# A vision transformer block on one core: for the first four images the unturned scores ahead of the turned ones, and the last q and k pair ahead of their denominators

## The chip, the cores and the metric

The kernel runs on one core of one Trainium2 chip. The metric is the device time of one execution in microseconds (us). Engines are named as in the profile: PE is TensorE (PEld its weight loads), DVE is VectorE, ACT is ScalarE, POOL is GpSimd, SP is SyncE, which only issues transfers here. Each engine runs its own instruction stream in order, and streams meet in semaphores.

## What is computed

A patch embedding with quantised weights gives 16 images of 37 tokens of width 256. On them stand an attention block and a mixture-of-experts attention block. The change lies in the first attention block. There, numerator and denominator come from two different sets of scores: the numerator from queries and keys turned by position (rotary), the denominator from the same queries and keys unturned. The causal mask is put on afterwards, on the numerator alone.

```python
qkv = x @ Wqkv                       # 16 heads of width 16
q_rot, k_rot = _rotate(q, cos, sin), _rotate(k, cos, sin)
num = jnp.exp(jnp.einsum('bhqd,bhkd->bhqk', q_rot, k_rot) * scale)
den = jnp.sum(jnp.exp(jnp.einsum('bhqd,bhkd->bhqk', q, k) * scale), axis=-1, keepdims=True)
attn = jnp.where(causal, num / den, 0.0)
y = jnp.einsum('bhqk,bhkd->bhqd', attn, v)
out = y @ Wout + bout
```

After it come residual, layer norm, the second block's q, k and gates, eight value experts, a second attention, and a sum over 32 pairs of head pair and expert (the long tail of the kernel, which the change does not touch).

## The kernel before

**Stages.** 0 to about 37 us: embedding, layer norm, turning of x. 34 to about 54 us: projections q, k, v of the first block. 48 to about 77 us: its attention, in four blocks `b` of four images. From there on: the second block, with PE nearly full to the end.

**Projections.** `PJ` lists twelve jobs in order, `NPJ` = 12: q and k of half 0 (images 0 to 7), 128 columns of the width at a time (jobs 0 to 3), v (4, 5), q and k of half 1, first 128 columns (6, 7), v (8, 9), q and k of half 1, second 128 columns (10, 11, "the last q and k pair"). They go to PSUM banks `PJB` = 0 to 7 and then 4 to 7 again. `proj_job(n)` is the PE part, `proj_read(n)` the ACT part (L575): for q and k two copies into `qun` or `kun` (L587), for v four into `vblk` (L596). Each adds one to `act_read`.

**Rotation.** `rope(r)` (L882) runs on DVE, once for each half and 128 columns: a shuffle, two products, a sum, and two writes each to `qrot` and `krot` (L899 to L906). It waits for ACT's read of its k job. `rope(0)` and `rope(1)` give what turned scores of blocks 0 and 1 need, `rope(2)` and `rope(3)` serve blocks 2 and 3.

**Attention of a block.** On PE: `scores(b, 0)` (turned) and `scores(b, 1)` (unturned), 32 matmuls each, both into banks 0 to 3, two banks for each half `t`; `attend(b)`, 64 small matmuls with v; `denominators(b)`, 8 records of matmuls with a matrix of ones. On ACT: `exps(b, 0)` into `en` (two buffers), `exps(b, 1)` into `ed` (one buffer), two instructions each (L648). On DVE: `causal(b)` masks `en` (L913, two instructions), `denominators(b)` takes the reciprocal (L930), `normalise(b)` writes `yT` (L935).

**Order on PE** (L1291 on): scores(0,0), job 10, job 11, scores(0,1), attend(0); scores(1,0), denominators(0), scores(1,1), attend(1); scores(2,0), denominators(1), scores(2,1), attend(2); scores(3,0), denominators(2), scores(3,1), output projection of the first groups (`out_proj`, L1274), denominators(3), more output projection, attend(3).

**Order on ACT** (L650 on): reads 0 to 9, exps(0,0), reads 10 and 11, exps(0,1), `ve_hi(0)` (an expert's weights rounded, L657), exps(1,0), exps(1,1), `ve_hi(1)`, exps of blocks 2 and 3.

**Order on DVE** (L918 on): rope(0), rope(1), rope(2), causal(0), rope(3); causal(1), denominators(0), normalise(0), causal(2), denominators(1), normalise(1), denominators(2), normalise(2), causal(3).

The order is written out by hand. `exp_ready` counts ACT's exponentials in the order in which they are issued, `s_ps` PE's halves of scores.

Of the kernel before, what the change touches and what calls it, by code (L numbers as in the profile page):

```python
# [23 lines left out]
KC = D // P  # L24
# [89 lines left out]
def vit_block(nc, x, tokw, vecs, consts, wqkv, wout, w2, ve, oe, mask_rows, out):  # L114
    with ExitStack() as ctx:
        def sem(name):
            return ctx.enter_context(nc.semaphore(name))
# [15 lines left out]
        NVR = 2  # L133
# [80 lines left out]
        qk = ExitStack()  # L214
# [8 lines left out]
        late = range(NOE, NOR)  # L223
# [30 lines left out]
        sm = {n: sem(n) for n in names}  # L254

        def cols(name, rows=P):
            a, b = _C[name]
            return cst[0:rows, a:b]
# [15 lines left out]
        def qk_set(hf, c):  # L274
            return [("qk", hf, c, kind) for kind in range(2)]

        PJ = qk_set(0, 0) + qk_set(0, 1) + [("v", m, 0, 0) for m in range(NV // 2)] + qk_set(1, 0)
        PJ += [("v", m, 0, 0) for m in range(NV // 2, NV)] + qk_set(1, 1)
        NPJ, NEARLY = len(PJ), KC * 2
        PJB = [0, 1] + [2, 3] + [4, 5] + [6, 7] + [4, 5] + [6, 7]  # L280
        PJPREV = [max([m for m in range(n) if PJB[m] == PJB[n]], default=-1) for n in range(NPJ)]
        RSTEPS = 8

        def act_reads(n):

            return n + 1

        def rope_reads(n):

            return RSTEPS * (len([j for j in PJ[:n] if j[0] == "qk"]) // 2) + 2  # L290

# [244 lines left out]
        def _(act):  # L536
# [38 lines left out]
            def proj_read(n):  # L575

                what, a, c, kind = PJ[n]
                act.wait_ge(sm["proj1_ps"], n + 1)
                if what == "qk":
                    if n == 0:  # L580

                        act.wait_ge(sm["qb_ready"], G)
                    im = slice(a * B // 2, (a + 1) * B // 2)
                    src = ps[:, PJB[n], 0:QH].rearrange("p (i s) -> p i s", s=SE)[:, :, 0:S]
                    for j in range(2):
                        dst = kun[:, c, im, DH2 * j:DH2 * j + S] if kind else qun[:, c, im, j]
                        ins = act.activation(dst, src, ACT.Copy, scale=cols("par")[:, (0 if kind else 4) + j:][:, 0:1])  # L587
                else:
                    if a == 0:

                        act.wait_ge(sm["vblk_zero"], 1)
                    for ii in range(2):
                        src = ps[DH2 * ii:DH2 * ii + S, PJB[n], :].rearrange("p (i a x) -> p i a x", a=2, x=P)
                        for p_ in range(2):
                            dst = vblk[DH2 * p_:DH2 * p_ + S, NVI * a + ii:NVI * (a + 1):2, :, p_]
                            ins = act.activation(dst, src[:, :, p_].rearrange("p i (h d) -> p i h d", d=DH1), ACT.Copy)  # L596
                ins.then_inc(sm["act_read"], 1)
# [36 lines left out]
            def exps(b, kind):  # L634

                if kind == 0 and b >= 2:
                    act.wait_ge(sm["pv_ps"], b - 1)
                if kind == 1 and b >= 1:
                    act.wait_ge(sm["den_ps"], b)
                for t in range(2):  # L640
                    act.wait_ge(sm["s_ps"], 4 * b + 2 * kind + t + 1)
                    src = ps[0:QR, 2 * t:2 * t + 2, 0:KC * 2 * JS * S]
                    if kind == 0:
                        dst = en[:, b % 2, t].rearrange("p r c i j s -> p r (c i j s)")
                    else:
                        src = src.rearrange("p r (c x) -> p r c x", c=KC)
                        dst = ed[:, :, :, 2 * t:2 * t + 2].rearrange("p r c i j s -> p r c (i j s)")
                    act.activation(dst, src, ACT.Exp, scale=DH1 ** -0.5).then_inc(sm["exp_ready"], 1)  # L648

            for n in range(NPJ - 2):  # L650
                proj_read(n)

            def ve_hi(e):
                act.wait_ge(ve_in[e % NVR], 16 * (e // NVR + 1))
                if e >= NVR:
                    act.wait_ge(sm["ve_ps"], NT * (e - NVR + 1))
                act.activation(vehi[:, e % NVR], veraw[:, e % NVR], ACT.Copy).then_inc(sm["vehi_ready"], 1)  # L657

            for b in range(NB):
                exps(b, 0)  # L660
                if b == 0:
                    proj_read(NPJ - 2)
                    proj_read(NPJ - 1)
                exps(b, 1)
                if b < NVR:
                    ve_hi(b)
            def x2_hi(g):

                act.wait_ge(sm["x2T_ps"], g + 1)
# [93 lines left out]
        def _(dve):  # L763
# [144 lines left out]

            def causal(b):
                for t in range(2):  # L910
                    dve.wait_ge(sm["exp_ready"], 4 * b + t + 1)
                    v = en[:, b % 2, t].rearrange("p r c i j s -> p (r c i j) s")
                    dve.tensor_tensor(v, v, bcast(cols("keep", QR), 1, 2 * KC * JP),  # L913
                                      ALU.mult).then_inc(sm["en_ready"], 1)
# [3 lines left out]
            rope(1)  # L918
            rope(2)
            causal(0)  # L920
            rope(3)

# [189 lines left out]
        def _(pe):  # L1112
# [101 lines left out]
            def scores(b, kind):  # L1214

                late = b * BI * 2 // B + 1
                pe.wait_ge(sm["keys_zero"], 2)
                pe.wait_ge(sm["rope_t"], RSTEPS * KC * late)
                pe.wait_ge(sm["act_read"], act_reads(PJ.index(("qk", late - 1, KC - 1, 1))))
                if b == kind == 0:  # L1220
                    bank_free(NEARLY - 1)
                for t in range(2):
                    if b + kind:
                        pe.wait_ge(sm["exp_ready"], 4 * b + 2 * kind + t - 1)
                    for ii in range(2):
                        i = b * BI + 2 * t + ii
                        for c in range(KC):
                            o = (c * 2 + ii) * JS * S
                            for r in range(RT):
                                rows = slice(r * P // RT, (r + 1) * P // RT)  # L1230
                                key = (kun if kind else krot)[rows, c, i]
                                qry = (qun if kind else qrot)[rows, c, i].rearrange("p a b -> p (a b)")
                                ins = pe.matmul(ps[0:QR, 2 * t + r, o:o + JS * S], key, qry, start=True, stop=True)  # L1233
                    ins.then_inc(sm["s_ps"], 1)

            def attend(b):
                if b < 2:
                    bank_free(NPJ - 3 if b == 0 else NPJ - 1)
                if b >= 2:
                    pe.wait_ge(sm["yT_ready"], b - 1)  # L1240
                for ii in range(BI):
                    if ii % 2 == 0:
                        pe.wait_ge(sm["en_ready"], 2 * b + ii // 2 + 1)
                    if b == NB - 1 and ii == 2:
                        turn_x2(0)
                    for c in range(KC):
                        u = c * BI + ii
                        for j in range(JP):
                            vv = vblk[:, b * BI + ii, c * JP + j].rearrange("p a b -> p (a b)")
                            ins = pe.matmul(ps[32 * j:32 * j + 32, 4 + 2 * (b % 2), u * S:(u + 1) * S], vv,  # L1250
                                            en[:, b % 2, ii // 2, j // JS, c, ii % 2, j % JS], start=True, stop=True)
                ins.then_inc(sm["pv_ps"], 1)

            def denominators(b):
                pe.wait_ge(sm["exp_ready"], 4 * b + 4)
                if b < 2:
                    bank_free(NPJ - 3 if b == 0 else NPJ - 1)
                if b >= 2:
                    pe.wait_ge(sm["yT_ready"], b - 1)
                for j in range(JP):  # L1260
                    ins = pe.matmul(ps[32 * j:32 * j + 32, 5 + 2 * (b % 2), 0:UN * S], cols("blk2", QR),
                                    ed[:, j // JS, :, :, j % JS], start=True, stop=True)
                ins.then_inc(sm["den_ps"], 1)
# [25 lines left out]
                ins.then_inc(sm["x2T_ps"], 1)  # L1289

            for b in range(NB):  # L1291
                scores(b, 0)
                if b == 0:
                    proj_job(NPJ - 2)
                    proj_job(NPJ - 1)
                else:
                    denominators(b - 1)
                scores(b, 1)
                if b == NB - 1:
                    out_proj(0)  # L1300
                    out_proj(1)
                    denominators(b)
                    for g in range(2, NOP):
                        out_proj(g)
                attend(b)
# [253 lines left out]
```

## Time and profile before

| what | value |
|---|---|
| runs | 240.1, 241.33, 242.55 us; median 241.33 |
| the profiled execution | 240.91 us, its span 238.4 us |
| mean granted clock of PE | 0.979 |
| PE busy | 207.9 us of the span (87%) |
| DVE busy | 178.7 us (75%) |
| ACT busy | 93.7 us (39%) |
| POOL busy | 79.5 us (33%) |

The span is the stretch in which the profile has instructions; 2.51 us of the profiled execution's time lie around it. The page divides the span into 40 slices and gives the busy share of each engine and the clock that was granted to PE. The chain that ended last is followed back from the last instruction: what stands in it sets the time, and what does not has slack. Idle time before an instruction comes with the instruction that ended it.

### The profile page before, as it was taken

To read this page: it belongs to the slowest core of one execution; us is meant where nothing else is said; L and a number is where in the kernel's file an instruction comes from. 1 tells how busy PE (TensorE), PEld (TensorE's weight loads), DVE (VectorE), ACT (ScalarE), POOL (GpSimd) and SP (SyncE) were. 2 spreads that over 40 slices of the span, in tenths; PEclk is the share of its full clock that TensorE was granted. 3 is DMA by queue.
4 is the path that set the end of the run, shared out by engine and by line. 5 is a ranking of instruction groups with operands and counts; after the bars stand their busy time and mean duration, and the time that the engine had idled before them with its cause. 6 is when DMAs were issued, how large, how long until landed. Compare 5 with 4: busy or idle time off the path is not lost.

```text
span 238.4 us, 5151 instructions
## 1 busy us (share of the span) xinstructions
PE 207.9 (87%) x2079; PEld 179.6 (75%) x2079; DVE 178.7 (75%) x324; ACT 93.7 (39%) x184; POOL 79.5 (33%) x82
## 2 busy tenths in 40 slices
PE   0153969689979799999999999999999999999994
PEld 0033849688865689987677777778989999999993
DVE  1679895998977767933558666775799979979972
ACT  3578739958741335445332155156202022110000
POOL 8562677000443424002253564955661000000000
PEclk9999999979999679999999999999999999999999
DMA  6998000000000010001602006067005435532102
GB/s 177 265 302 322 2 0 4 0 3 3 3 3 3 18 71 3 0 0 29 252 3 88 3 12 254 0 181 201 3 7 185 120 123 172 165 95 61 44 0 103
DMA packets 7181, 19.56 MB, mean 82 GB/s; under 512 B 1043, under 2 KB 1878, under 8 KB 7030
## 3 DMA queue, kind: packets, MB, share of 16 engines
q1 hardware_dynamic: 7158, 19.24, 26.3%
q8 instruction: 16, 0.26, 0.5%
q14 instruction: 7, 0.06, 0.1%
HBM read 18.55 MB, written 0.68 MB: 81 GB/s over the span
## 4 chain that ended last, share of the span: by engine, by line
PE 49%; DVE 28%; issue 9%; ACT 4%; POOL 4%; DMA 4%; SPq 1%; DVEq 0%; ACTq 0%; POOLq 0%
PE ps L265 13%; PE ps L266 11%; PE ps L267 11%; DVE gx L1101 7%; DMA tw<-tok_weight 4%; PE ps L1233 3%; PE ps L1274 2%; PE ps L1434 2%; DVE oelo L1075 2%; DVE rden L930 2%; DVE amax L774 1%; PE ps L1404 1%; ACT ptb L720 1%; DVE stat L803 1%; POOL velo L485 1%
## 5 line engine op out<-in xcount | busy, mean ns | idle before, releaser
L1101 DVE TENSOR_TENSOR gx<-maskb,oT 128x1184 fp32r<-128x1184 bf16 x31 | 42.3, 1414 | 0.6 <-PE ps L267 0.6
L1038 DVE COPY_PREDICATED v<-onehot,ps 128x512 f32<-128x512 uint8 (+3 forms) x40 | 25.7, 661 | 17.6 <-PE ps L267 17.3
L265 PE MATMUL ps<-gx,oelo 128*128 128x296 f32 x124 | 37.8, 305 | 0.6 <-DVE gx L1101 0.6
L267 PE MATMUL ps<-gx,oehi 128*128 128x296 f32 x124 | 37.2, 300 | 0.0
L266 PE MATMUL ps<-gx,oehi 128*128 128x296 f32 x124 | 37.0, 298 | 0.0
L265 PE MATMUL ps<-vehi,x2lo 128*128 128x512 f32 (+3 forms) x90 | 35.2, 392 | 0.0
L266 PE MATMUL ps<-velo,x2hi 128*128 128x512 f32 (+3 forms) x90 | 33.3, 370 | 0.0
L267 PE MATMUL ps<-vehi,x2hi 128*128 128x512 f32 (+3 forms) x90 | 33.2, 369 | 0.0
L485 POOL TENSOR_TENSOR velo<-veraw,vehi 128x1024 fp32r<-128x1024 f32 x8 | 19.1, 2390 | 23.8 <-ACT vehi L657 17.3
L265 PEld LDWEIGHTS ps<-gx,oelo 128*128 128x128 f32 x124 | 23.3, 188 | 1.8 <-issue 1.3
L266 PEld LDWEIGHTS ps<-gx,oehi 128*128 128x128 f32 x124 | 23.4, 189 | 0.0
L267 PEld LDWEIGHTS ps<-gx,oehi 128*128 128x128 f32 x124 | 23.3, 188 | 0.0
L1137 PE MATMUL ps<-ident_bf,qb 111*128 111x111 bf16 x36 | 4.5, 297 | 17.3 <-DVE qb L799 17.2
L265 PEld LDWEIGHTS ps<-vehi,x2lo 128*128 128x128 f32 (+1 forms) x90 | 16.2, 180 | 4.2 <-issue 0.7
L267 PEld LDWEIGHTS ps<-vehi,x2hi 128*128 128x128 f32 (+1 forms) x90 | 16.2, 180 | 3.7
L266 PEld LDWEIGHTS ps<-velo,x2hi 128*128 128x128 f32 (+1 forms) x90 | 16.2, 180 | 2.8
L1137 PEld LDWEIGHTS ps<-ident_bf,qb 111*128 111x128 bf16 x36 | 3.1, 139 | 19.3 <-DVE qb L799 19.1
L728 ACT ACTIVATE oehi<-oeraw 128x1024 fp32r<-128x1024 f32 x8 | 8.5, 1064 | 18.7 <-DMA oeraw<-output_w 18.7
L457 POOL TENSOR_TENSOR rstd<-lnv,half_neg 111x1 f32<-111x1 f32 x12 | 7.9, 659 | 17.7 <-DVE lnv L805 17.7
L707 ACT ACTIVATE pe<-sc 101x444 f32<-101x444 f32 (+1 forms) x6 | 3.2, 534 | 24.5 <-POOL sc L500 24.5
L452 POOL TENSOR_TENSOR w2lo<-w2raw,w2hi 128x544 fp32r<-128x544 f32 x4 | 5.3, 1344 | 21.8 <-DVE en L913 20.8
L265 PE MATMUL ps<-x2hi,w2lo 128*128 128x296 f32 x32 | 11.0, 345 | 0.1
(165 smaller groups left out, 479.8 us busy)
## 6 DMA issues: line engine op xcount, KB each, us to landing
maskb<-mask_rows SPq DMA_DIRECT2D x32, 148.0 KB, 3.9
veraw<-value_w SPq DMA_DIRECT2D x8, 512.0 KB, 3.7
oeraw<-output_w SPq DMA_DIRECT2D x8, 512.0 KB, 4.0
xp<-x_rows SPq DMA_DIRECT2D x6, 336.0 KB, 9.9
w2raw<-w_qkgate SPq DMA_DIRECT2D x1, 1088.0 KB, 14.1
tw<-tok_weight SPq DMA_DIRECT2D x1, 768.0 KB, 8.4
wqraw<-w_qkv SPq DMA_DIRECT2D x1, 768.0 KB, 12.0
out<-yo SPq DMA_DIRECT2D x4, 148.0 KB, 1.9
```

The source lines that it names most:

```text
L265: pe.matmul(o, llo, rhi, start=start, stop=False)
L266: pe.matmul(o, lhi, rlo, start=False, stop=False)
L267: return pe.matmul(o, lhi, rhi, start=False, stop=stop)
L452: pool.tensor_tensor(w2lo[:, n // 2, part], w2raw[:, n // 2, part], w2hi[:, n // 2, part].bitcast(F32), ALU.subtract).then_inc(sm["w2lo_re ...
L457: pool.tensor_tensor(rstd[:, which, g:g + 1], lnv[:, which, g:g + 1], half_neg[0:R, 0:1], ALU.pow).then_inc(sm["rstd_ready"], 1)
L485: pool.tensor_tensor(velo[:, e % NVR], veraw[:, e % NVR], vehi[:, e % NVR].bitcast(F32), ALU.subtract).then_inc(sm["velo_ready"], 1)
L728: act.activation(oehi[u % NOR][:], oeraw[RAW[u]][:], ACT.Copy).then_inc(sm["oehi_ready"], 1)
L930: dve.reciprocal(rden[:], ps[:, 5 + 2 * (b % 2), 0:UN * S]).then_inc(sm["rden_ready"], 1)
L1038: dve.copy_predicated(v2[0:m, t, h0:h1], bcast(onehot[0:m, t, h0:h1, e], 2, DH2), ps[0:m, JBANK[n], 0:(h1 - h0) * DH2].rearrange("p (a b) ...
L1101: dve.tensor_tensor(gx[:, k % NGR].rearrange("p a b t -> p a (b t)"), bcast(maskb[:, w % NMR, k % MEU], 1, 2), oT[:, c % 2].bitcast(F32), ...
L1137: ins = pe.transpose(dst[:, c * (R + 1):c * (R + 1) + R], qb[:, g % NQB, c * P:(c + 1) * P], ident_bf[0:R, 0:R])
L1233: ins = pe.matmul(ps[0:QR, 2 * t + r, o:o + JS * S], key, qry, start=True, stop=True)
```

## The change

On PE, unturned scores of block 0 are issued first, then the turned ones, then jobs 10 and 11, then denominators(0). The turned attend(0) moves behind scores(1,0), to where denominators(0) stood. On ACT, exps(0,1) comes after read 8, then read 9, exps(0,0), reads 10 and 11; `ve_hi(0)` and `ve_hi(1)` move behind exps(1,1) and exps(2,1). DVE's order is as before. `unit(b, kind)` numbers the half-blocks in the new order of issue, and the waits on `s_ps` and `exp_ready` follow it. Unturned scores wait neither for `rope_t` nor for the second `keys_zero` any more.

```diff
+        def unit(b, kind):
+
+            return 2 * b + (kind if b else 1 - kind)
+
...
-                    act.wait_ge(sm["s_ps"], 4 * b + 2 * kind + t + 1)
+                    act.wait_ge(sm["s_ps"], 2 * unit(b, kind) + t + 1)
...
-            for n in range(NPJ - 2):
+            for n in range(NPJ - 3):
                 proj_read(n)
+            exps(0, 1)
+            proj_read(NPJ - 3)
+            exps(0, 0)
+            proj_read(NPJ - 2)
+            proj_read(NPJ - 1)
...
             for b in range(NB):
-                exps(b, 0)
-                if b == 0:
-                    proj_read(NPJ - 2)
-                    proj_read(NPJ - 1)
-                exps(b, 1)
-                if b < NVR:
-                    ve_hi(b)
+                if b:
+                    exps(b, 0)
+                    exps(b, 1)
+                if 1 <= b <= NVR:
+                    ve_hi(b - 1)
...
-                    dve.wait_ge(sm["exp_ready"], 4 * b + t + 1)
+                    dve.wait_ge(sm["exp_ready"], 2 * unit(b, 0) + t + 1)
...
-                pe.wait_ge(sm["keys_zero"], 2)
-                pe.wait_ge(sm["rope_t"], RSTEPS * KC * late)
-                pe.wait_ge(sm["act_read"], act_reads(PJ.index(("qk", late - 1, KC - 1, 1))))
-                if b == kind == 0:
+                u = unit(b, kind)
+                if kind:
+                    pe.wait_ge(sm["keys_zero"], 1)
+                    pe.wait_ge(sm["act_read"], act_reads(PJ.index(("qk", late - 1, KC - 1, 1))))
+                else:
+                    pe.wait_ge(sm["keys_zero"], 2)
+                    pe.wait_ge(sm["rope_t"], RSTEPS * KC * late)
+                if u == 0:
                     bank_free(NEARLY - 1)
                 for t in range(2):
-                    if b + kind:
-                        pe.wait_ge(sm["exp_ready"], 4 * b + 2 * kind + t - 1)
+                    if u:
+                        pe.wait_ge(sm["exp_ready"], 2 * u + t - 1)
...
-                pe.wait_ge(sm["exp_ready"], 4 * b + 4)
+                pe.wait_ge(sm["exp_ready"], 2 * unit(b, 1) + 2)
...
             for b in range(NB):
-                scores(b, 0)
                 if b == 0:
+                    scores(0, 1)
+                    scores(0, 0)
                     proj_job(NPJ - 2)
                     proj_job(NPJ - 1)
+                    denominators(0)
+                    continue
+                scores(b, 0)
+                if b == 1:
+                    attend(0)
                 else:
                     denominators(b - 1)
                 scores(b, 1)
```

## Rows read from the trace of the kernel before

**Rows 1.** The page, part 1: busy us (share of the span), instructions.
```profile
PE 207.9 (87%) x2079; PEld 179.6 (75%) x2079; DVE 178.7 (75%) x324; ACT 93.7 (39%) x184; POOL 79.5 (33%) x82
```

**Rows 2.** The chain that ended last, in order of time: start, us, what.
```profile
45.85 2.45 issue
48.30 2.47 PE ps L1233 x32
...
52.58 0.91 ACT qun L587 x2
53.49 0.89 ACT kun L587 x2
...
58.95 1.32 DVE en L913 x2
...
60.30 0.48 PE ps L1250 x32
...
66.99 0.70 PE ps L1261 x8
```

**Rows 3.** DVE in order of time: start, us, line, operation, idle before and its releaser.
```profile
44.57 0.76 DVE L900 TENSOR_TENSOR ropet<-ps,cst 128x592 f32<-128x592 f32 x1
...
47.55 0.65 DVE L906 TENSOR_SCALAR krot<-ropet,cst 128x296 f32<-128x296 f32 x2
...
52.41 1.46 DVE L913 TENSOR_TENSOR en<-en,cst 101x592 f32<-101x592 f32 x2
...
54.41 0.01 DVE L899 LOAD_MASK_SELECT partner<-ps  x1 [0.54 <-ACT kun L587]
...
65.99 0.47 DVE L935 TENSOR_TENSOR yT<-ps,rden 128x296 f32<-128x296 f32 x1
67.78 2.01 DVE L930 RECIPROCAL rden<-ps 128x296 f32<-128x296 f32 x1 [1.32 <-PE ps L1261]
```

**Rows 4.** ACT in order of time, columns as for DVE above.
```profile
45.22 3.11 ACT L596 ACTIVATE vblk<-ps 37x256 f32<-37x256 f32 x8
49.45 0.66 ACT L648 ACTIVATE en<-ps 101x592 f32<-101x592 f32 x1 [1.12 <-PE ps L1233]
...
60.15 1.05 ACT L657 ACTIVATE vehi<-veraw 128x1024 fp32r<-128x1024 f32 x1
```

**Rows 5.** PE in order of time, columns as for DVE above.
```profile
51.62 0.46 PE L265 MATMUL ps<-x1hi,wqlo 128*128 128x304 f32 x1
51.88 0.46 PE L266 MATMUL ps<-x1lo,wqhi 128*128 128x304 f32 x1
...
52.52 0.31 PE L266 MATMUL ps<-x1lo,wqhi 128*128 128x304 f32 x1
52.67 0.32 PE L267 MATMUL ps<-x1hi,wqhi 128*128 128x304 f32 x1
...
53.35 1.65 PE L1233 MATMUL ps<-qun,kun 64*101 64x74 f32 x32
54.93 0.78 PE L1250 MATMUL ps<-en,vblk 101*32 101x37 f32 x64
...
57.24 0.72 PE L1261 MATMUL ps<-ed,cst 101*32 101x296 f32 x8
...
70.44 1.95 PE L1274 MATMUL ps<-wo,yT 128*111 128x256 f32 x8 [1.21 <-DVE yT L935]
...
81.90 3.73 PE L1274 MATMUL ps<-wo,yT 128*111 128x256 f32 x8 [0.75 <-DVE yT L935]
```

**Rows 6.** Windows: stretch, its length, busy us of PE, PEld, DVE, ACT, POOL, PE's clock, DMA.
```profile
45.85:48.30 2.45, 0.00 (x1) 0.03 (x1) 2.38 (x8) 2.37 (x7) 0.00 (x0) 1.00 0.00 0
...
48.93:50.77 1.84, 1.84 (x25) 1.71 (x21) 1.77 (x4) 0.66 (x1) 0.00 (x0) 0.50 0.04 9
...
69.22:70.44 1.22, 0.01 (x2) 0.03 (x1) 1.19 (x3) 0.71 (x2) 0.00 (x0) 1.00 0.00 0
76.24:79.65 3.41, 2.28 (x26) 1.73 (x16) 2.30 (x8) 1.73 (x7) 0.88 (x2) 1.00 0.02 5
...
48.93:52.35 3.42, 3.42 (x30) 3.29 (x27) 3.32 (x8) 1.33 (x2) 0.00 (x0) 0.50 0.02 5
79.65:86.48 6.83, 6.08 (x19) 4.85 (x19) 4.36 (x9) 0.44 (x2) 2.68 (x2) 0.50 0.24 77
```

## Prediction

> **What bounds the kernel now.** I read the page first: PE is busy for 87% of the span, DVE for 75%, ACT for 39% [rows 1]. That average says little about 15 us out of 238, so the rest goes by the stretch from 45 to 72 us, in this order: the chain, the three engines in order of time, then the windows with PE's clock.
>
> The chain [rows 2] shows two things in this stretch. PE stands still for 2.45 us from 45.85, because turned scores need `rope(1)`, which DVE ends at 48.20 [rows 3]. And the chain then goes PE (scores, job 10) to ACT (the reads of jobs 10 and 11, the last ending at 54.38) to DVE (`rope(3)`, whose successor, the mask of block 1, starts at 58.95) to PE (attend(1) at 60.30) and through the scores to denominators(2) at 66.99, which releases the reciprocal at 67.78.
>
> The reader is to see how thin the first part of that chain is. DVE ends the mask of block 0 at 52.41 + 1.46 = 53.87 and waits only 0.54 us before `rope(3)` [rows 3]. Within 45.85 to 48.30 DVE is busy for 2.38 of 2.45 us [rows 6]. So up to 59 us it is DVE that bounds the stretch, and PE's idle 2.45 us lie beside it. After `rope(3)` the order is reversed: DVE ends its own work at 65.99 + 0.47 = 66.46 and waits 1.32 us for PE [rows 3]. From 59 to 67 us PE sets the end, with DVE 1.32 us behind it.
>
> The windows [rows 6] show the clock. After PE's idle 2.45 us it was granted half (1.2 of 2.4 GHz) for 3.42 us, 48.93 to 52.35. After a stretch in which PE was busy for 2.28 of 3.41 us, it was granted half for 6.83 us. After an idle 1.22 us from 69.22 it did not fall.
>
> **The change, part by part.** It removes and adds no matmul, exponential or transfer; the queues of SP and POOL keep their order. What it moves:
>
> 1. *Unturned scores into the gap.* They need reads 0 to 3 and the second step of `rope(1)` (bank 2 and 3 free), which ends at 44.57 + 0.76 = 45.33 [rows 3]. So PE starts at 45.85 and takes 1.65 us for 32 matmuls at full clock [rows 5]: until 47.5. Then it is idle until `rope(1)` ends, 0.8 us instead of 2.45. An idle 1.22 us brought no fall [rows 6], so the turned scores run 48.30 to 49.95 at full clock, where they took 2.47 us before [rows 2].
>
> 2. *Reads on ACT.* Eight copies of v take 3.11 us from 45.22 [rows 4], four of them until 46.8. exps(0,1), two of 0.66 us, wait for the second half of the scores (47.5) and end at 48.2. Read 9, four copies, until 49.8. exps(0,0) until 51.1. Jobs 10 and 11, twelve matmuls at 0.15 us start to start (52.52 to 52.67) [rows 5], end near 51.8 on PE. Reads 10 and 11 take 0.91 + 0.89 us [rows 2]: 51.1 to 52.9. DVE is free for `rope(3)` at 53.87, so this is hidden by 1.0 us. DVE's wait of 0.54 us goes. That is the whole gain on the engine that bounds the stretch: 0.54 us. The mask of block 0 has its exponentials at 51.1, before 52.41, so it isn't late.
>
> 3. *What PE does next.* denominators(0), 0.7 us [rows 5], 51.8 to 52.4 (read 9, whose bank it needs, is over at 49.8). scores(1,0) until 54.1. attend(0), 0.78 us [rows 5], until 54.8: both masks are there at 53.87. scores(1,1) until 56.4; its exps(1,0) on ACT are over at 54.9. Then comes attend(1), which needs the mask of block 1. DVE gives its first half at 58.95 - 0.54 + 0.7 = 59.1. So PE stands still from 56.4 to 59.2, 2.8 us. The gap is not closed: it moves from before the scores to before attend(1), and in the kernel before PE was nearly without a gap there. What is late next is queued behind attend(1) on PE: scores(2,0), and after it everything to denominators(2), for which DVE waits.
>
> 4. *`ve_hi` on ACT.* Each takes 1.05 us [rows 4]. Behind exps(2,1), which end near 65.3, `ve_hi(1)` ends where exps(3,0) start (66.4); ACT has nothing else there. Value 0, bound from above by 1.05 us.
>
> 5. *The clock behind the moved gap.* The trace of before has no such gap here, so I bound it. Below, 0: the idle 1.22 us without a fall [rows 6]. Above, from the nearest row: idle 2.45 us, then 3.42 us at half clock. The new gap is longer than that, so I take a fall. Its price: turned scores lost 2.47 - 1.65 = 0.82 us, of which 1.84 us were at half clock [rows 2, 5, 6]: 0.45 us lost for each us at half clock. A fall that lies wholly in work costs 3.42 x 0.45 = 1.5 us; one that begins a us earlier costs 1.0 us, since part of it lies in the gap. About 0.3 us is absorbed, because attend(1)'s first half waits for the second half of the mask anyhow. Value 1.15 us. This lies on the chain: PE was the last to come at 67.78, and DVE's cover of 1.32 us is on DVE's side. Before, the fall lay under DVE's work and showed only as the wait of 0.54 us.
>
> The Trainium skill ("TensorE: Matmul & The Clock Gate", section Terms) prices a throttled time at this time x (1 - K/N), that is one half at 1.2 of 2.4 GHz. That would be 1.7 us and a sum of +1.2 us; the row of the scores shows a smaller loss, 0.45, and I go by the row.
>
> **Sum.** -0.54 (wait of DVE) + 1.15 (half clock on the chain) = +0.6 us. The profiled execution took 240.91 us, so 241.5. It was 0.42 us faster than the median 241.33, and for the median I say 241.9.
>
> **The rivals.**
>
> *No fall behind the gap* (-0.5 us, 240.8). For it: 1.22 us idle brought none. Against: 2.45 us did, and the new gap is 2.8. If `rope(3)` started no earlier, this would be +-0. That would be the change not doing what it says; against it stands the 1.0 us of slack on ACT in step 2.
>
> *The half clock lasts on* (slower). The second fall of before lasted 6.83 us [rows 6]. If the one behind the moved gap did too, it would cover PE from 59.2 on to denominators(2): 6.6 us x 0.45 = 3.0, less 0.54: +2.4, 243.7. It decides (over 1%) from 2.4 us on. Against it: the first fall ended after 3.42 us, with PE busy throughout, as it would be here; in the long one PE was idle again (6.08 busy of 6.83 us).
>
> *A later fall lands elsewhere* (faster). The output projection took 3.73 us at 81.90 and 1.95 us at 70.44 for the same eight records [rows 5], and it is on the chain. If a shift in time moved that fall away, 1.8 us and the matmuls behind it, about 0.6 us, would be spared: 241.9 - 2.4 = 239.5. For it: the three runs of the unchanged kernel are 2.45 us apart, which is about the size of such a fall. Against: nothing in the change thins or thickens PE's work there.
>
> *ACT becomes the gate of the rotation.* exps(0,1) now stand ahead of reads 9 to 11. It would need more than 1.0 us of delay; with the 0.54 us not gained and a fall paid: +1.15, 242.5. It is inside the range.
>
> **How the numbers follow.** Forecast (a fall, paid once, ACT as gate or not) 0.62; no fall 0.18; half clock for twice as long 0.11; the later fall spared 0.09. A measurement of this kernel can tell about 1% (2.4 us) from no change. The forecast's own spread is 1.0 to 1.5 less 0.54, +0.3 to +1.2, widened by the runs' own spread of 1.2 us to each side: 240.6 to 243.4. The range reaches down to the case without a fall less half of that spread: 240.0 to 243.3. Faster by over 1% gets 0.09, nearly all from the later fall and from the median of few runs; slower 0.13, from the long fall and the upper end of the forecast; within 1% the rest, 0.78.
>
> **What would show it.** Step 1: unturned scores at 45.9, turned ones at 48.3 in 1.65 us. Step 2: DVE's wait before `rope(3)` gone, exps(0,0) ending at 51.1. Step 3: a PE idle time of 2.8 us ahead of attend(1), ended by the mask. Step 5: half clock after it, scores(2,0) at 2.5 us or more, DVE's wait for denominators(2) at 1.3 + 1.15 = 2.5 us instead of 1.32. I am wrong if the clock stays full there (then DVE waits 1.3 us and the time is 0.5 us under before), if reads 10 and 11 end after 53.9, or if the stretch after 72 us, where the change touches nothing, differs by more than the stretch before it.

## The result, and the profile after

The changed kernel takes 247.31 us in the median of six runs (246.22 to 247.62); the kernel before takes 240.77 us (238.61 to 242.55) beside it. The ratio is 1.0286, with a 95% interval of 1.0239 to 1.0332. I had forecast 241.9 us and no change that can be told. Ratios leave out runs more than 1.5% above the fastest of the same kernel, and what moves the runs here moves them by as much; so medians of all runs stand beside them below, and for two experiments the single runs.

The profiled execution took 247.30 us, its span is 244.4 us. The page shows the place. This is its row of the clock granted to PE, in 40 slices of 6.1 us:

```profile
PEclk9999999997555959999999999999999999999999
```

Slices 10 to 13 stand at 7, 5, 5, 5: a stretch of about 20 us at half clock that the kernel before does not have. (The 5 in slice 15 is a later fall; the kernel before has it too, 79.65 to 86.48 [rows 6].) The windows of the changed kernel give its ends (columns as in [rows 6]: length, busy us of PE, PEld, DVE, ACT and POOL, clock, DMA):

```profile
56.00:58.53 2.53, 0.00 (x1) 0.03 (x2) 2.50 (x8) 1.51 (x2) 0.00 (x0) 0.84 0.00 0
57.90:78.30 20.40, 19.77 (x280) 16.13 (x280) 11.32 (x12) 6.25 (x9) 5.31 (x4) 0.50 0.01 2
...
59.00:78.30 19.30, 19.30 (x264) 15.63 (x255) 10.22 (x11) 6.25 (x9) 5.31 (x4) 0.50 0.01 2
```

PE is idle in the first window, and the clock falls within it. Look at the last row: from 59.0 to 78.3 us PE is busy for 19.30 of 19.30 us, and the clock stays at half (1.2 of 2.4 GHz) all the same. The first 16.4 us behind the gap, 58.53 to 74.92, are attention work alone; then comes the output projection, and the clock rises 3.3 us into it, at 78.2. In the kernel before, this attention work ran at full clock [rows 5]. PE of the changed kernel in order of time:

```profile
45.20 1.65 PE L1244 MATMUL ps<-qun,kun 64*101 64x74 f32 x32
47.72 1.65 PE L1244 MATMUL ps<-qrot,krot 64*101 64x74 f32 x32 [0.87 <-DVE krot L913]
...
54.20 1.65 PE L1244 MATMUL ps<-qun,kun 64*101 64x74 f32 x32
58.53 1.31 PE L1261 MATMUL ps<-en,vblk 101*32 101x37 f32 x64 [2.68 <-DVE en L920]
59.77 3.00 PE L1244 MATMUL ps<-qrot,krot 64*101 64x74 f32 x32
62.70 1.21 PE L1272 MATMUL ps<-ed,cst 101*32 101x296 f32 x8
63.84 3.00 PE L1244 MATMUL ps<-qun,kun 64*101 64x74 f32 x32
66.78 1.22 PE L1261 MATMUL ps<-en,vblk 101*32 101x37 f32 x64
67.92 3.00 PE L1244 MATMUL ps<-qrot,krot 64*101 64x74 f32 x32
70.85 1.21 PE L1272 MATMUL ps<-ed,cst 101*32 101x296 f32 x8
72.00 3.00 PE L1244 MATMUL ps<-qun,kun 64*101 64x74 f32 x32
74.92 3.59 PE L1285 MATMUL ps<-wo,yT 128*111 128x256 f32 x8
78.44 0.72 PE L1272 MATMUL ps<-ed,cst 101*32 101x296 f32 x8
```

Up to 54.2 us everything is at its full rate, and both gaps are where the order puts them: 0.87 us ahead of the turned scores, 2.68 us ahead of attend(1). Behind the second gap each set of scores takes 3.00 us instead of 1.65, denominators 1.21 instead of 0.72, attend 1.22 instead of 0.78 [rows 5]. The output projection takes 3.59 us instead of 1.95, and only behind it is the next denominators record back at 0.72. PE was the engine that set the end there, so this shows in the waits between 45 and 80 us (who for whom, total, times, longest):

```profile
DVE rden L937 <- PE ps L1272: 5.5, 1, 5.5
...
PE ps L1261 <- DVE en L920: 2.7, 1, 2.7
```

DVE waits 5.5 us for denominators(2), where it had waited 1.32 us [rows 3].

The sum, counted from the end of the v projections (45.85 us before, 45.20 after; these 0.65 us arise ahead of the first instruction that the change moves): the mask of block 1 starts 13.10 us later before [rows 2] and 12.55 after (57.75 in the chain of the changed kernel), 0.55 us gained. The output projection starts 24.59 us later before [rows 5] and 29.72 after, 5.1 us lost. The projection itself loses 1.6 more. That makes 6.8 us behind it, and at the end of the span it is 6.65 (238.4 - 45.85 = 192.55 against 244.4 - 45.20 = 199.2). So the whole loss arises between 58 and 78.5 us, and the stretch behind it, which the change leaves alone, adds nothing.

### The profile page after: what moved, and what is told of

Its sections match the earlier page's. It is cut to its first block, busy times and chain, and to the rows that moved or that the text cites. A ratio compares the mean times of both kernels' runs of the same rounds, so it can differ in the third digit from the quotient of the medians.

```text
span 244.4 us, 5144 instructions
## 1 busy us (share of the span) xinstructions
PE 214.4 (88%) x2079; PEld 184.8 (76%) x2079; DVE 178.7 (73%) x324; ACT 93.4 (38%) x184; POOL 78.7 (32%) x82
## 4 chain that ended last, share of the span: by engine, by line
PE 46%; DVE 34%; issue 8%; ACT 5%; POOL 4%; DMA 1%; DVEq 0%; POOLq 0%; ACTq 0%
PE ps L265 10%; PE ps L267 9%; PE ps L266 9%; DVE gx L1108 7%; PE ps L1244 5%; PE ps L1285 3%; PE ps L1451 2%; DVE oelo L1082 2%; DVE stat L810 2%; DVE amax L781 1%; DVE ropet L909 1%; DMA xp<-x_rows 1%; DVE partner L906 1%; PE ps L1421 1%; DVE ropex L908 1%
## 5 line engine op out<-in xcount | busy, mean ns | idle before, releaser
L489 POOL TENSOR_TENSOR velo<-veraw,vehi 128x1024 fp32r<-128x1024 f32 x8 | 19.1, 2387 | 23.8 <-ACT vehi L666 17.3
L937 DVE RECIPROCAL rden<-ps 128x296 f32<-128x296 f32 x4 | 8.0, 2003 | 5.5 <-PE ps L1272 5.5
```

The lines of the kernel that those rows point to most:

```text
L489: pool.tensor_tensor(velo[:, e % NVR], veraw[:, e % NVR], vehi[:, e % NVR].bitcast(F32), ALU.subtract).then_inc(sm["velo_ready"], 1)
L937: dve.reciprocal(rden[:], ps[:, 5 + 2 * (b % 2), 0:UN * S]).then_inc(sm["rden_ready"], 1)
```

## The experiments

The theory: the gap ahead of attend(1) brings the clock down, attention work does not bring it up again, and this is the whole loss. The rivals: the new order makes an engine late by itself; the low stretch has a length of its own; only the place of attend(0) matters.

**Filling the gap with dense work.** 17 matmuls of the shape of a projection, into a bank that is free at that time:

```diff
+            def dense(n, bank):
+                for _ in range(n):
+                    pe.matmul(ps[:, bank, 0:QH].rearrange("p (i s) -> p i s", s=SE), wqhi[:, 0, 0, 0:P],
+                              x1hi[:, 0, 0:B // 2, 0:SE], start=True, stop=True)
...
+                if b == 1:
+                    bank_free(NPJ - 1)
+                    dense(17, 7)
                 attend(b)
```

> The changed kernel, with 17 projection-shaped matmuls (128x304 columns, result not used) into a free bank between scores(1,1) and attend(1), where PE stood still for 2.7 us. Theory (the fall of the clock in that gap, kept up because attention work does not lift it, is the whole loss): granted clock 1.00 from 57.9 to 78.3 us, scores 1.65 us each, DVE's wait for denominators(2) about 1.3 instead of 5.5 us, time about 0.5 us under the kernel before, 240.3 us (238.5 to 242). Rival (the new order itself makes PE or ACT late): the clock is full but the time stays above 244 us.

Measured: 239.99 us in the median of 12 runs (238.04 to 241.44), the kernel before 241.25; ratio 0.9994 (0.9948 to 1.0040). All 12 runs have a mean granted clock of 0.981 or more, where five of the changed kernel's six had 0.944. PE and the windows of this run:

```profile
55.86 2.79 PE L1250 MATMUL ps<-x1hi,wqhi 128*128 128x304 f32 x17
58.61 1.07 PE L1274 MATMUL ps<-en,vblk 101*32 101x37 f32 x64
59.60 1.65 PE L1244 MATMUL ps<-qrot,krot 64*101 64x74 f32 x32
```

```profile
55.86:78.50 22.64, 20.20 (x399) 16.00 (x398) 19.13 (x37) 9.97 (x19) 7.48 (x8) 1.00 0.01 2
78.70:85.30 6.60, 5.66 (x18) 4.43 (x17) 4.12 (x9) 0.42 (x1) 2.39 (x2) 0.50 0.24 79
```

Full clock from the gap to 78.5 us, and DVE waits 1.2 us for denominators(2). Nothing else was changed, so the 7.3 us between the two medians (1.0286 and 0.9994 of the kernel before) are the clock's, and the rival in which the order makes PE or ACT late falls. The half microsecond that I had counted as gain can't be told from zero by this interval.

**Filling it with thin work.** The same place, with matmuls of the shape of the scores:

```diff
+            def light(n, bank):
+                for k in range(n):
+                    rows = slice(k % 2 * P // RT, (k % 2 + 1) * P // RT)
+                    pe.matmul(ps[0:QR, bank + k % 2, 0:JS * S], kun[rows, 0, 0],
+                              qun[rows, 0, 0].rearrange("p a b -> p (a b)"), start=True, stop=True)
...
+                    light(50, 6)
```

> The changed kernel, with 50 matmuls of the shape of the scores (64 rows, 74 columns, result not used) in the same gap. Theory that only standing still brings the fall: as with the dense filler, about 240.3 us. Theory that what counts is how much of the array is fed (the scores did not lift the clock once it was low): here it could fall all the same, and stay low until the output projection, about 247 us. The attention stretch of the kernel before ran on such work at full clock, so I expect 240.3 us, with 0.65.

Measured: 240.85 us (239.98 to 241.77, 10 runs), ratio 1.0014 (0.9975 to 1.0053). No fall at the gap. The filler was sized wrongly: one fp32 matmul is two records (so a set of scores, x32, is 16 matmuls and not 32), and 50 of them took 4.62 us, 1.9 more than the gap. With 28 it fits:

> light_gap with 28 instead of 50 score-shaped matmuls in the gap: 50 took 4.6 us, 1.9 us more than the gap, and stood on the chain with them; 28 take 2.6 us. Theory (work that does not lift a low clock still keeps a full one): no fall, and the 1.9 us come back, 1 us or more under light_gap, as dense_gap, ratio 0.997 to 1.000. Rival (with idle remainders around it the light filler is too thin): some runs at 247 us.

```profile
56.35 2.66 PE L1257 MATMUL ps<-qun,kun 64*101 64x74 f32 x56
59.18 1.06 PE L1274 MATMUL ps<-en,vblk 101*32 101x37 f32 x64 [0.17 <-DVE en L920]
60.17 1.65 PE L1244 MATMUL ps<-qrot,krot 64*101 64x74 f32 x32
```

Measured: 239.38 us (237.99 to 240.03, 4 runs), the kernel before 241.99; ratio 0.9905 (0.9883 to 0.9928). That the ratio is lower than with dense work is no merit of thin work: all seven runs of the kernel before beside it had a clock of 0.967 to 0.970, the four of this kernel 0.986 to 1.00, and the profiled one has no later fall either. What the run shows is the clock at the gap. So this fall comes only where PE stands still. Thin work in its place keeps the full clock, though the same thin work did not raise a low one.

**Dense work behind the gap.** The gap stays, and 12 projection-shaped matmuls stand behind attend(1):

```diff
                 attend(b)
+                if b == 1:
+                    dense(12, 7)
```

> The changed kernel, gap left as it is, and 12 projection-shaped matmuls right behind attend(1), 3 us at half clock of work that is not needed. Theory (a low clock is lifted by dense work, not by attention work): the clock rises within 3 to 7 us of the gap instead of 20, and the time falls in spite of the added 3 us: 3 us added, some 4 to 5.5 us given back, about 245.5 us (244 to 246.5). Rival (the low stretch has a length of its own, or attention work would lift it sooner or later): low until about 78 us as before, and 3 us more, 250 us.

```profile
58.42 1.31 PE L1274 MATMUL ps<-en,vblk 101*32 101x37 f32 x64 [2.65 <-DVE en L920]
59.66 2.93 PE L1250 MATMUL ps<-x1hi,wqhi 128*128 128x304 f32 x12
62.52 1.65 PE L1244 MATMUL ps<-qrot,krot 64*101 64x74 f32 x32
```

```profile
58.45:61.80 3.35, 3.35 (x72) 3.25 (x73) 2.88 (x3) 0.00 (x0) 1.34 (x1) 0.50 0.02 5
61.80:90.00 28.20, 24.02 (x364) 19.22 (x364) 20.34 (x44) 10.91 (x24) 9.96 (x10) 1.00 0.06 20
```

Measured: 243.04 us (240.31 to 244.29, 10 runs), ratio 1.0092 (1.0049 to 1.0135). The gap of 2.65 us brings the fall again, but with dense work behind it the low stretch lasts 3.35 us instead of 20.4, and 2.9 us of useless work make the kernel 4.3 us faster than the changed one. It is 2.5 us better than I had expected and outside my 244 to 246.5; I had allowed the rise up to 7 us. The profiled run is the fastest of the ten, 240.31 us at a clock of 0.993, and has no later fall. The other nine had 0.970 to 0.986, so they spent more time at half clock, and no trace shows where. The rival with a length of its own falls. This is the experiment that names my error (below).

**Undoing one part.** attend(0) and denominators(0) back in their old places:

```diff
                     proj_job(NPJ - 1)
-                    denominators(0)
+                    attend(0)
                     continue
                 scores(b, 0)
-                if b == 1:
-                    attend(0)
-                else:
-                    denominators(b - 1)
+                denominators(b - 1)
```

> The changed kernel, with attend(0) and denominators(0) back in the places they had before, one behind jobs 10 and 11, the other behind scores(1,0); only the scores, exps and ve_hi stay moved. Theory (the gap comes from PE being ahead of DVE's rotation, whatever the order of its work): PE idle about 2.5 us ahead of attend(1), clock low until the output projection, 247 us. Rival (the moved attend(0) matters): under 245 us.

Measured: four runs, 248.04 and 247.93 us at a mean granted clock of 0.944 and 0.943, 238.43 and 238.30 us at 1.00. The median of 243.18 describes none of them. The profile is of a long run:

```profile
52.73 1.07 PE L1261 MATMUL ps<-en,vblk 101*32 101x37 f32 x64 [1.42 <-DVE en L920]
53.73 2.12 PE L1244 MATMUL ps<-qrot,krot 64*101 64x74 f32 x32
...
56.92 3.00 PE L1244 MATMUL ps<-qun,kun 64*101 64x74 f32 x32
```

```profile
54.80:78.60 23.80, 23.80 (x332) 19.43 (x329) 14.34 (x19) 9.77 (x14) 5.31 (x4) 0.50 0.01 1
```

With attend(0) in front, PE waits for the mask of block 0 already: 1.42 us, idle time that would otherwise lie ahead of attend(1). A long fall came in two of four runs, and in the profiled one the clock then stayed at half for 23.8 us. It did not fall in the idle time but 2.0 us behind it, at 54.8, with PE busy in between. I was wrong to expect it always. The idle 1.22 us of [rows 6], which I took for safe in the prediction, is one case in one trace; 1.42 us is little more. Why the fall comes in one run and not in another stays open. For the rival of attend(0) this says that its place is not the cause, since the long fall came with it in its old place, but that it can decide whether the fall comes: with attend(0) moved, none of six runs was without it. The two short runs, at a clock of 1.00, have no later fall either, so the 9.6 us between the two pairs are not the price of the long fall alone. Both halves filled with eight dense matmuls each:

> The kernel attend_back with 8 projection-shaped matmuls ahead of attend(0) and 8 ahead of attend(1) (results not used), which fill the two idle times into which its gap is split. attend_back had runs at granted clock 1.00 and 238.4 us and runs at 0.944 and 248.0 us. Theory (the fall alone divides them): all runs in the group near 238 to 240 us, none at 248, ratio 0.99 to 1.00. Rival (something else divides them): some runs at 248 us again.

Measured: 239.98 us (237.65 to 241.32, 12 runs), ratio 0.9959 (0.9912 to 1.0007). No run lies near 248.

**A part of the gap.** Six dense matmuls instead of 17:

> dense_gap with 6 matmuls instead of 17 ahead of attend(1): PE idle about 1.8 us there instead of 2.7 (changed kernel) or 0. Theory that a part of the gap is enough for some runs: two groups of runs, at 247 to 248 us with a long fall and at 238 to 241 us without, since attend_back, with idle times of 1.4 and about 1.3 us, had both. Rival (1.8 us idle is short enough): all runs under 242 us.

```profile
58.79 1.22 PE L1274 MATMUL ps<-en,vblk 101*32 101x37 f32 x64 [1.60 <-DVE en L920]
59.94 3.00 PE L1244 MATMUL ps<-qrot,krot 64*101 64x74 f32 x32
```

Measured: four runs, 246.54, 247.35, 240.31 and 244.94 us, at clocks of 0.956, 0.944, 0.986 and 0.958; the kernel before 241.99. An idle 1.60 us can bring the fall as well, in three of four runs by their times and clocks. In the profiled one it came 0.75 us behind the idle time, at 59.5.

**The first fall of the kernel before.** 15 dense matmuls in its idle 2.45 us, ahead of the turned scores:

```diff
             for b in range(NB):
+                if b == 0:
+                    bank_free(1)
+                    dense(15, 0)
                 scores(b, 0)
```

> The kernel before, with 15 projection-shaped matmuls (result not used) in PE's idle 2.45 us ahead of the turned scores of block 0. Theory (the first fall of the kernel before is mostly hidden behind DVE, of it only DVE's wait of 0.54 us ahead of rope(3) is on the chain): granted clock 1.00 from 48 to 53 us, that wait gone, 0.5 us faster, ratio 0.998. Rival (the first fall cost its full price of 1.4 us on PE): ratio 0.994.

Measured: 239.80 us (238.02 to 241.62, 12 runs), the kernel before 241.42; ratio 0.9984 (0.9941 to 1.0026). The windows show full clock there:

```profile
45.00:53.00 8.00, 7.75 (x96) 7.25 (x94) 7.79 (x18) 6.47 (x16) 0.00 (x0) 1.00 0.01 2
```

The times do not decide: the ratio lies on the value of the hidden fall, 0.998, but its interval reaches down to the rival, and the medians of all runs lie 1.6 us apart, nearer to the rival's 1.4. The traces do. DVE's wait ahead of rope(3) is gone, and the reciprocal that waits for denominators(2) starts 20.2 us behind the last write of rope(1) in the kernel before (67.78 - 47.55 [rows 3]) and 19.6 us behind it here (66.87 - 47.24). So the first fall cost 0.6 us where it reaches the chain. Removing it is worth less than 1%, while the fall at the next place cost 2.9%.

**The later fall.** Both output projections, turn 1, turn 2 and the first gate job get dense matmuls ahead of them (6, 3, 1, 1 and 5), in the kernel before and on top of dense_gap:

```diff
+                    pe.wait_ge(sm["yT_ready"], NB - 2)
+                    dense(6, 7)
                     out_proj(0)
...
             for kind, n in D_ORDER:
+                dense({("turn", 1): 3, ("turn", 2): 1, ("gate", 0): 1, ("out", 4): 5}.get((kind, n), 0), 1)
```

> The kernel before with only the later fillers of all_gaps (ahead of both output projections, turn 1, turn 2 and the first gate job), its first fall left as it is. Theory (the later fall costs 2.4 us where it comes, and the spread of the kernel before from 238.1 to 243.3 us is mostly that fall coming or not): no fall after 60 us, runs within 1 us of each other, near 238.5 to 239 us, ratio 0.99. Rival: the later fall is hidden, ratio 1.00.

> The changed kernel with the dense filler of the first run ahead of attend(1), and more of it where PE waits later: 6 matmuls ahead of the first output projection, 3, 1 and 1 ahead of turn 1, turn 2 and the first gate job, 5 ahead of the last output projection (results not used). Theory (the later fall of 6.8 us costs 1.8 us in the output projection and about 0.6 behind it, and is brought by thin work on PE from 75 us on): no fall at all, clock 1.00, 2 to 2.4 us under dense_gap, 238 us, ratio to the kernel before 0.99. Rival (the added matmuls stand on the chain themselves, 5 us in all at 0.15 each where a wait was shorter than they are): ratio 1.00.

Measured: before_late 239.20 us (237.88 to 240.26), ratio 0.9970 (0.9931 to 1.0008); all_gaps 237.63 us (237.05 to 238.77), ratio 0.9887 (0.9854 to 0.9921), 12 runs each, the kernel before at 241.42. all_gaps came out as expected, 2.4 us under dense_gap. before_late missed: I had expected a ratio of 0.99 and runs within 1 us of each other, and they are 2.4 us apart (those of the kernel before 4.7), with an interval that holds the rival's 1.00; the medians of all runs are 2.2 us apart. Its profiled run has no fall after 60 us, but six of its 12 have a clock of 0.985 or 0.986, twice the time at half clock of the profiled one with its 0.993, and no trace shows where. That the later fall has a price at all rests on dense_gap and all_gaps, which differ in the later fillers alone and whose intervals lie apart; before_late by itself doesn't show it. all_gaps:

```profile
79.93 0.89 PE L1250 MATMUL ps<-x1hi,wqhi 128*128 128x304 f32 x5
81.44 1.95 PE L1298 MATMUL ps<-wo,yT 128*111 128x256 f32 x8 [0.62 <-DVE yT L942]
```

```profile
37.00:236.00 199.00, 192.03 (x2010) 167.49 (x2008) 152.14 (x251) 70.53 (x146) 57.98 (x49) 1.00 0.20 66
```

No fall in these 199 us (the clock was at half once before, 33.1 to 36.5 us, ahead of the change), and the last output projection takes 1.95 us instead of 3.73 [rows 5]. all_gaps beats both kernels: 1.1% under the one before, 9.7 us under the changed one, with 33 matmuls whose result nobody uses. Its runs are 1.7 us apart, those of the kernel before 4.7 us (238.08 to 242.77), and there time and clock go together in the main: four runs at 0.993 have a median of 238.7 us, six at 0.979 one of 241.6.

## Why the prediction was wrong

*Step 1* held: unturned scores at 45.20 us, turned ones 1.65 us long behind an idle 0.87.

*Step 2* held: DVE starts `rope(3)` right behind the mask of block 0, and the mask of block 1 comes 0.6 us earlier.

*Step 3* held nearly to the number: 2.68 us idle ahead of attend(1) where I had 2.8, ended by the mask.

*Step 4* held: `ve_hi` moved without a cost that shows.

*Step 5 failed*, and in its duration alone: the term "1.15 (half clock on the chain)" of the sum measured 7.5. The fall came, the rate of loss was as I had read it (3.00 against 1.65 us for a set of scores: 1.35 lost in 3.00, 0.45 for each us), and it lay on the chain. I took the 3.42 us that the first fall of before had lasted as the length of this one too. It lasted 20.4 us. Added up over the records between 58.5 and 78.5 us at half clock: four sets of scores 1.35 each, two denominators 0.49 each, attend(2) 0.44, attend(1) some 0.2, the output projection 1.64, together 8.7 us. The 1.21 us for which PE had waited ahead of the output projection in the kernel before cover a part; 7.5 are left, less the 0.54 gained 6.9, against 6.8 in the trace.

The step went wrong at one sentence, the argument against the second rival: "with PE busy throughout, as it would be here". Busy was the wrong thing to read. In the 3.42 us behind the first fall stood the rest of the turned scores and then job 10, matmuls over the full array, and the clock rose 1.65 us into it (50.70 to 52.35 us). The change moves these jobs to the other side of the gap. Behind it stands attention work only, 64 rows or 32 columns of the array at a time, and 16.4 us of it did not raise the clock. dense_behind put dense work back there, and the low stretch was 3.35 us long again. Two other traces agree: 21.3 us of attention work at half clock in attend_back and 15.5 us in gap_6, and the clock rose 2.5 and 1.5 us into the output projection that followed, where the changed kernel's rose 3.3 us into it. What in the dense work counts was not separated, as rows, columns and the length of each matmul change together. That an fp32 matmul runs as two records is not it: the output projection does so too (four matmuls, x8).

So the second rival, half clock for longer, is what happened. It had a chance of 0.11 and a price of 2.4 us, because I ended its low stretch after 6.83 us, the longest in the trace. Had I asked which work ended each low stretch, I would have found a projection at both (the end of job 10, and the q and k jobs behind the last output projection), and would have run this one on to the first output projection: about 20 us. The second of them is also a warning: the whole last output projection stood in it at half clock, from 81.90 us on, and the clock rose only at 86.48 [rows 5, 6]. So dense work does not end a low clock at once, nor always equally soon.

The Trainium skill ("TensorE: Matmul & The Clock Gate", section "What's actually happening") says that activity releases the throttle, which is set by how busy the PE has been recently. Here PE busy from end to end was not enough by itself: it was busy for 19.3 of 19.3 us before the clock rose.

Two figures of the prediction do not follow from its own terms. 1.0 to 1.5 us less the 0.3 absorbed gives 0.7 to 1.2, so that 1.15 is the upper end and not the middle; and 1.0 to 1.5 less 0.54 is +0.5 to +1.0, not +0.3 to +1.2. Both are small beside the miss.

The order of engines that I had read off was right, and it explains why a fall cost 0.6 us in one place (by the traces of before_gap) and so much more in the other, beyond its longer duration: at 49 us DVE sets the end and PE has slack, from 59 us on it is the reverse.

## What to carry to other kernels

When an idle gap of an engine with a gated clock is moved, look at what stands behind it: dense matmuls ended a low clock within a few us here, small attention matmuls left it low for as long as they lasted. Read a low stretch by the work that ended it, not by its length. Where a gap can't be closed, matmuls with an unused result can hold the clock, and no cost of them could be told here where they were about as long as the wait (dense_gap: 2.79 us for a wait of 2.68).

## What the runs showed of the hardware

- A clock at half was not raised by 16.4 us of uninterrupted attention matmuls (64x74, 101x37 and 101x296 in fp32) in the changed kernel, nor by 21.3 us of them in attend_back, but 12 matmuls of 128x304 close behind the fall were followed by full clock 3.35 us after it. At full clock the same attention work ran from 53.35 to 69.22 us in the kernel before without a fall.
- The fall came behind idle times of 2.65 and 2.68 us, behind 1.60 us in three runs of four, and in two runs of four where the gap was split and 1.42 us stood first. It did not come where 2.66 us of thin matmuls filled the gap. The clock fell within the idle time in the changed kernel, but 0.6 us behind it in the kernel before, 0.75 us in gap_6 and 2.0 us in attend_back, with PE busy again.
- At half clock a set of 32 score records takes 3.00 us against 1.65, 64 attend records 1.22 against 0.78: less than double, where projection matmuls go from 0.15 to 0.25 us start to start [rows 5].
